# Sixteen row numbers to a read, and column tiles ten slots apart on VectorE, in a three-layer graph network

## What is computed

```python
out = x @ W_root + b
x_src = x[src]
for r in range(R):
    mask = (edge_type == r).astype(x.dtype)
    agg = jax.ops.segment_sum(x_src * mask[:, None], dst, num_segments=n)
    cnt = jax.ops.segment_sum(mask, dst, num_segments=n)
    mean = agg / jnp.maximum(cnt, 1.0)[:, None]
    out = out + mean @ W[r]
```

## Time and profile before

| | us |
|---|---|
| median of the runs (3105.36 to 3108.71) | 3106.48 |
| the profiled execution's own time | 3107.02 |
| its span | 3105.2 |
| busy: GpSimd / TensorE / VectorE / ScalarE | 2234.3 / 2077.3 / 1813.1 / 1463.8 |
| layer two: first and last gather of GpSimd start at | 1105.85 / 2066.82 |
| layer two: last evacuation of ScalarE starts at | 2073.99 |
| layer three: last gather / last evacuation start at | 3056.15 / 3063.64 |

### The profile page before, as it was taken

How to read it: one execution, slowest core, us unless ns; L and a number is a source line. 1 busy time by engine, 2 the same in 40 slices (tenths; PEclk the granted TensorE clock), 3 DMA queues, 4 the chain that set the end, 5 groups by cost and what they waited for, 6 DMA issues and landing times. The chain is left out here.

```text
span 3105.2 us, 100185 instructions
## 1 busy us (share of the span) xinstructions
PE 2077.3 (67%) x13106; PEld 1917.0 (62%) x13106; DVE 1813.1 (58%) x10398; ACT 1463.8 (47%) x9497; POOL 2234.3 (72%) x2361
## 2 busy tenths in 40 slices
PE   7977777777767666665566666666666666566566
PEld 6856666666666545665565666665565556556566
DVE  5545544445444346666666666664666666666665
ACT  1132222222222156666666666645666666666664
POOL 6647777777777657777777777747777777777772
PEclk9988888889888777777877767787777777777778
DMA  3112222222222132222222222222222222222232
GB/s 105 50 33 56 56 56 56 56 56 56 56 56 56 47 90 56 56 56 56 56 56 56 56 55 56 56 77 62 56 56 56 56 56 55 56 56 56 56 96 64
DMA packets 117512, 182.61 MB, mean 59 GB/s; under 512 B 45039, under 2 KB 76242, under 8 KB 116850
## 3 DMA queue, kind: packets, MB, share of 16 engines
q0 software_dynamic: 75072, 153.90, 19.1%
q1 hardware_dynamic: 39510, 21.71, 2.5%
q10 hardware_dynamic: 2268, 0.59, 0.1%
HBM read 166.42 MB, written 9.60 MB: 57 GB/s over the span
## 5 line engine op out<-in xcount | busy, mean ns | idle before, releaser
L478 POOL DMA_INDIRECT ring<-node_table,src_t x1536 | 1455.5, 948 | 524.5 <-issue 372.6
L1265 PE MATMUL ps_a<-onehot,ring 128*128 128x128 f32 x4992 | 874.1, 330 | 888.8 <-PEq L302 793.1
L1265 PEld LDWEIGHTS ps_a<-onehot,ring 128*128 128x128 f32 x4992 | 760.6, 233 | 953.5 <-issue 858.0
L688 DVE TENSOR_SCALAR onehot<-iota,key,weight 128x128 f32<-128x128 f32 x2496 | 886.7, 369 | 351.5 <-DVEq L302 344.1
L964 ACT COPY act_cols<-h_t 128x1 f32 x8448 | 897.4, 187 | 396.6 <-issue 375.4
L478 POOL DMA_INDIRECT ring<-in_x,src_t x810 | 776.3, 958 | 297.7 <-issue 187.7
L1275 PE MATMUL ps_o<-sums,w_rel 128*128 128x128 f32 x4992 | 925.9, 364 | 61.0 <-PEq L302 60.8
L1275 PEld LDWEIGHTS ps_o<-sums,w_rel 128*128 128x128 f32 x4992 | 904.3, 280 | 69.8 <-issue 69.4
L993 ACT COPY sums<-ps_a 128x512 f32<-128x512 f32 x624 | 365.7, 586 | 912.5 <-ACTq L302 865.3
L712 DVE COPY dve_cols<-h_t 128x1 f32 x4608 | 552.4, 154 | 414.6 <-issue 246.1
L699 DVE TENSOR_TENSOR out_t<-out_t,ps_o 128x16 f32 x2496 | 439.1, 176 | 46.2 <-DVEq L302 28.0
(11 more groups left out here) (148 smaller groups left out, 587.9 us busy)
## 6 DMA issues: line engine op xcount, KB each, us to landing
ring<-node_table SPq DMA_DIRECT2D x3328, 0.5 KB
ring<-in_x SPq DMA_DIRECT2D x1792, 0.5 KB
ring<-node_table,src_t POOLq DMA_INDIRECT x1536
ring<-in_x ACTq DMA_DIRECT2D x1024, 0.5 KB
ring<-in_x,src_t POOLq DMA_INDIRECT x810
node_table<-ring SPq DMA_DIRECT2D x24, 256.0 KB
out_rows<-ring SPq DMA_DIRECT2D x12, 256.0 KB
w_rel<-in_L_gnn_Ws SPq DMA_DIRECT2D x3, 512.0 KB
```

The source lines that it names most:

```text
L478: nc.gpsimd.indirect_dma_start(out=ring[:, q % G, t, :], out_offset=None, in_=source, in_offset=bass.IndirectOffsetOnAxis(ap=src_t[:, q * ...
L688: ins = nc.vector.tensor_scalar(onehot[:, b, t, :], iota_1[:, :], key[:, col:col + 1], weight[:, col:col + 1], ALU.is_equal, ALU.mult)
L1265: ins = nc.tensor.matmul(ps_a[b][:, t * KEYS:(t + 1) * KEYS], ring[:, q % G, t, :], onehot[:, b, t, :], start=True, stop=True)
```

## The change

`LOADS` stays at 8 for the rows that SyncE and ScalarE fetch by DMA. The column copies of layers two and three use a new `WIDE = 16`: one call reads 16 row numbers, then 16 columns are copied, and a tile has 8 batches instead of 16. `column_tiles` places the 8 batches over the same `steps`. VectorE's `steps` goes from 11 to 10, which gives 20 tiles a layer instead of 18; the two more are no longer fetched by GpSimd (766 gathers a layer instead of 768). ScalarE keeps 6 and its 33 tiles. In ScalarE's six slots now stand 2, 1, 1, 2, 1, 1 batches of 16; in VectorE's ten 1, 1, 1, 1, 0, 1, 1, 1, 1, 0. The last copies of VectorE lie in slot 198 instead of 197.

```diff
-COLUMNS = {"act": (GT - 2, (0, 6)), "dve": (GT - 3, (0, 11))}
+WIDE = 16
+COLUMNS = {"act": (GT - 2, (0, 6)), "dve": (GT - 3, (0, 10))}
...
-        at = [first + k * steps * LOADS // P for k in range(P // LOADS)]
+        at = [first + k * steps * WIDE // P for k in range(P // WIDE)]
...
-                node = load_value(dve, dve_row_idx[0:1, b, e:e + LOADS], 0, N - 1,
+                node = load_value(dve, dve_row_idx[0:1, b, e:e + WIDE], 0, N - 1,
                                   "the graph's edges join its nodes")
-                for j in range(LOADS):
+                for j in range(WIDE):
                     ins = nc.vector.tensor_copy(dve_cols[:, b, e + j:e + j + 1], h_t[:, bass.ds(node[j], 1)])
-                if e + LOADS == P:
+                if e + WIDE == P:
                     ins.then_inc(dve_cols_ready, 1)
...
-                    for k in range(P // LOADS):
+                    for k in range(P // WIDE):
                         if at[k] == q:
-                            copy_columns(n, k * LOADS)
+                            copy_columns(n, k * WIDE)
```

More of the change, by code:

```diff
@@ L960, in copy_columns @@
                     take(act, act_step)
-                node = load_value(act, act_row_idx[0:1, b, e:e + LOADS], 0, N - 1,
+                node = load_value(act, act_row_idx[0:1, b, e:e + WIDE], 0, N - 1,
                                   "the graph's edges join its nodes")
-                for j in range(LOADS):
+                for j in range(WIDE):
                     ins = nc.scalar.copy(act_cols[:, b, e + j:e + j + 1], h_t[:, bass.ds(node[j], 1)])
-                if e + LOADS == P:
+                if e + WIDE == P:
                     ins.then_inc(act_cols_ready, 1)
```

## The result

| | before | after |
|---|---|---|
| median of the runs, us | 3107.6 (3105.36 to 3110.13) | 3172.62 (3171.33 to 3173.55) |
| ratio to before, 95% interval | | 1.0209 (1.0191 to 1.0226) |
| profiled execution, its span, us | 3107.02, 3105.2 | 3173.55, 3171.7 |

The before column counts four runs, one more than stood ahead of the prediction. The changed kernel is 65.0 us slower, where 60 were forecast (3167); the interval is 59 to 70 us, so it holds the 60. It has one line more at its head, so L688 of before is L689 here, L712 is L713, and so on.

The account below looks back on a forecast made before the run. VectorE was taken to bound layers two and three by a little, GpSimd some microseconds behind; net +30.1 us a layer, +60 in both, on 3107.02 gave 3167 us. Range 3092 to 3181, the forecast's own 3155 to 3180.

Parts of the forecast that it names:

- VectorE bounds, GpSimd a few us behind it: Layers two and three: VectorE's instruction stream sets the slot, 4.68 us, against GpSimd's pace of 4.63 us.
- The price of a read of 16: VectorE's read of 16 row numbers into registers: estimated at 1.10 us, 1.13 with what lies around it.
- a step for each group of four: VectorE's register reads: each further four numbers add 0.252 us, as seen from 4 to 8 numbers.
- the pair that the argument rested on: VectorE's reads of 4 and 8 numbers, 0.345 and 0.597 us, extended in a straight line to 16.
- break-even point: VectorE's read of 16: at 0.91 us, 0.94 with what lies around it, gain and loss cancel.
- The sum: VectorE's stream, one layer: reads removed 181.4 us, added 180.8, copies 29.4, landings and waits 1.3; net +30.1 us.
- The spread of VectorE's batches changes no sum: VectorE's ten slots, two of them without any batch: claimed to add nothing to the time.
- The lumps of ScalarE: ScalarE's 32 copies in every third slot: evacuation some 1 us late, priced 0, at most 1 us each six slots.
- A read of 16 at the price of one of 8: Rival on VectorE's reads: 0.63 to 0.69 us each, GpSimd becomes the bound, 3095.5 us; chance 0.31.
- Two reads of 8: Rival on VectorE's reads: the call comes out as two shorter reads, 3208 us; chance 0.10.
- The third rival: GpSimd is the bound already and VectorE just keeps up: 3102 us if reads stay cheap; chance 0.02.

Follow-up runs that it names:

- half_read_steps10: The changed kernel, but VectorE reads only 8 row numbers for 16 column copies and uses each twice: 3097.96 us, 0.9968 of before.
- wide16_steps12: The changed kernel with VectorE's tiles 12 slots apart instead of 10, 16 tiles a layer: 3105.06 us, 0.9996 of before.
- act16_only: The kernel before with reads of 16 on ScalarE alone, VectorE left at reads of 8 and 11 slots: 3108.63 us, 1.0007 of before.

## Why the prediction was right

- **VectorE bounds, GpSimd a few us behind it.** Right, and shown from both sides. Shortening VectorE's stream, by 19 us a layer or by far more, gained 6 to 8 us and no more. With much less work TensorE waits for gathered rows through the whole layer (half_read_steps10, wide16_steps12), with 19 us less only toward its end. Lengthening the stream by 35 us a layer (reads of four) cost 70.
- **The price of a read of 16.** Right to 1 ns (1.10 and 1.099), and that close only by luck, as two points can't tell a law and the picture behind it was rough: a step for each group of four holds only for whole groups that begin on a multiple of four. All reads of row numbers in the two kernels are of that kind. So was the pair that the argument rested on, 4 and 8 numbers on the same engine. The read of one number (0.32) isn't, and a line through it and the read of eight gives 0.91, just the break-even point.
- **The sum.** Two more tiles and the reads: forecast 2 x (29.4 - 0.6) = 57.6 us, measured 56.5 in the row of the copies. The reads are even but for a few us: 320 of 1.099 are 351.7 us, 576 of 0.597 were 343.9.
- **What was left out.** "The spread of VectorE's batches changes no sum" looked wrong by 14.1 us in the row of `weigh`. With the copies spread these gaps stood before other instructions and the time stayed within its noise, so the sentence holds to a few us. The 5 us between forecast and result are inside the interval, and no run gives them a cause. The lumps of ScalarE, priced at 0, were rightly 0 within the 5 us that act16_only leaves open.
- **The break-even point.** A read of 0.91 us. On one side 1.10 gave 3172 for the forecast 3167; on the other half_read_steps10 gave 3098 for 3095, but there the copies were shorter too. No run stands near 0.91, so the point itself is not shown.
- **Rivals.** A read of 16 at the price of one of 8 would by the sum have made the kernel faster; it costs 1.099 us and not 0.6 to 0.7. Two reads of 8 did not happen. The third rival, GpSimd as the bound already, falls: the engine with 70% in the changed kernel was spared two gathers a layer for nothing, while the one with 59% set the time, because that share leaves out the reads that its sequencer does. By the Trainium skill, page "Perfetto Trace Analysis", section "Identifying the Most-Contended Engine", the engine with the highest occupancy is the one to optimise first; this case's traces disagree.

What beats both kernels is the change without its second half: reads of 16, tiles left 11 slots apart, 0.9978 of before, or 0.9986 with reads of 16 on VectorE alone.

## What to carry to other kernels

An engine's busy share leaves out what its sequencer does; where register reads and waits fill the gaps, add them up before calling the engine idle, and see who is late at the end of the stage. When an idle time grows in one row, look whether it shrank in another before giving it a price. A longer read into registers saves little (0.12 us for each read that falls away here), so don't spend the saving on more work before it is measured. And move an engine's load only as far as the next bound: here GpSimd's was 6 to 8 us away, and everything beyond it was lost. When something is taken away to test a price, check in the trace that nothing else went with it.

## What the runs showed of the hardware that was not expected

A read of row numbers into VectorE's registers takes 0.345, 0.597, 0.844, 1.10 and 2.10 us for 4, 8, 12, 16 and 32 numbers that begin on a multiple of 16 bytes, but 0.312, 0.539 and 0.758 for 1, 2 and 3, and 2.075 to 3.392 us for 9, 10, 11, 13, 14 and 15 numbers that begin elsewhere. A read of fifteen numbers off such a place costs as much as three reads of sixteen on it. And sixteen column copies in a row take 1.87 us with sixteen registers, but 1.44 us with eight used twice.
